# Linear attention: the output bias is added to x by GpSimd after queries and keys have unit length, and three dummy products stand in front of the first transposes

## The reference, cut to what matters

```python
x = x + _L0_attn_a_ref(_layernorm(x, axis=-1), Wq, bq, Wk, bk, Wv, bv, Wo, bo, projection)

def _spherical_features(x, projection):
    x_norm = x / (jnp.linalg.norm(x, axis=-1, keepdims=True) + 1e-08)
    return jax.nn.relu(jnp.einsum('bhsd,hfd->bhsf', x_norm, projection)) + YAT_EPS
...
Q, K, V = heads(x @ Wq + bq), heads(x @ Wk + bk), heads(x @ Wv + bv)   # 16 heads of 8
Qp, Kp = _spherical_features(Q, projection), _spherical_features(K, projection)
QKV = jnp.einsum('bhsf,bhfd->bhsd', Qp, jnp.einsum('bhsf,bhsd->bhfd', Kp, V))
normalizer = jnp.einsum('bhsf,bhf->bhs', Qp, jnp.sum(Kp, axis=2))[..., None]
out = QKV / jnp.maximum(normalizer, 1e-06)
return out.reshape(b, s, EMBED_DIM) @ Wo + bo
```

## Time and profile before

| | us |
|---|---|
| median of 3 runs | 953.96 |
| the profiled execution | 953.76 |
| its span, first to last instruction | 951.9 |
| PE busy in the span | 828.7 |
| DVE busy | 664.3 |
| ACT busy | 555.1 |
| POOL busy | 198.3 |

### The profile page before, as it was taken

One profiled execution on the slowest core, in us unless ns is written; L12 is line 12 of the kernel. 1 busy time (PEld: TensorE's weight loads), 2 busy tenths in 40 slices (PEclk: granted clock), 3 DMA queues, 4 the chain that ended last, 5 costly groups with the idle time before them and its releaser, 6 DMA issues.

```text
span 951.9 us, 17381 instructions
## 1 busy us (share of the span) xinstructions
PE 828.7 (87%) x6615; PEld 530.3 (56%) x6615; DVE 664.3 (70%) x1288; ACT 555.1 (58%) x1205; POOL 198.3 (21%) x177
## 2 busy tenths in 40 slices
PE   4889937799999889999999999999995899895894
PEld 2579735599956543333333333333575598594694
DVE  5855884266567999999999999992427364566362
ACT  2451542155525856999999888899644254423252
POOL 2000037455500050000000000000112454205385
PEclk9999957999999999999999999999996799995897
DMA  4750001321130000000000000000230212000444
GB/s 122 200 142 1 1 14 48 106 67 35 38 91 1 1 1 1 2 1 2 1 2 2 1 2 1 2 2 1 89 91 15 90 39 75 2 1 31 125 36 71
DMA packets 54643, 36.86 MB, mean 39 GB/s; under 512 B 9138, under 2 KB 50162, under 8 KB 54546
## 3 DMA queue, kind: packets, MB, share of 16 engines
q1 hardware_dynamic: 47218, 25.98, 9.8%
q0 software_dynamic: 7344, 9.77, 4.4%
HBM read 22.31 MB, written 14.48 MB: 39 GB/s over the span
## 4 chain that ended last, share of the span: by engine, by line
DVE 33%; PE 32%; POOL 14%; issue 11%; DMA 4%; ACT 4%; SPq 1%; POOLq 0%; DVEq 0%; ACTq 0%
DVE arena L1634 22%; POOL slots L1147 7%; POOL results L1158 5%; PE psum L1718 4%; PE psum L1687 2%; POOL results L1169 2%; PE psum L1251 2%; ACT arena L1898 2%; PE psum L280 2%; PE psum L402 2%; PE psum L380 2%; PE psum L1781 2%; PE psum L1769 1%; PE psum L1616 1%; PE psum L440 1%
## 5 line engine op out<-in xcount | busy, mean ns | idle before, releaser
L1634 DVE TENSOR_REDUCE arena<-psum 128x2 f32<-128x1024 f32 x256 | 294.1, 1220 | 8.6 <-PE psum L1616 8.6
L1898 ACT ACTIVATE arena<-psum 128x512 f32<-128x512 f32 x512 | 266.7, 606 | 18.9 <-PE psum L1687 16.7
L1294 ACT ACTIVATE arena<-psum,arena 128x128 f32<-128x128 f32 x340 | 97.2, 369 | 122.2 <-PE psum L1261 65.7
L1718 PE MATMUL psum<-arena 128*32 128x256 f32 (+1 forms) x1920 | 159.6, 405 | 0.2 <-ACT expert_w L1879 0.2
L1687 PE MATMUL psum<-arena 32*128 32x512 f16 x512 | 127.3, 384 | 1.8 <-ACT arena L1898 0.4
L287 PE MATMUL psum<-la_wqkv,ident 128*128 128x384 f32 x336 | 123.5, 518 | 2.4 <-ACT arena L1998 2.0
L1616 PE MATMUL psum<-arena 32*128 32x512 f16 x512 | 100.6, 384 | 17.1 <-DVE arena L1634 15.1
L1147 POOL DMA_INDIRECT slots<-xn,arena x64 | 66.4, 1038 | 196.0 <-DVE arena L1371 177.4
L1251 PE MATMUL psum<-arena 128*128 128x128 f32 x680 | 97.0, 288 | 0.7 <-DVE arena L1452 0.6
L287 PEld LDWEIGHTS psum<-la_wqkv,ident 128*128 128x128 f32 x336 | 65.1, 202 | 52.2 <-issue 15.4
L1261 PE MATMUL psum<-arena 128*128 128x128 f32 x680 | 89.9, 275 | 1.0 <-ACT arena L1294 1.0
(11 more groups left out here) (279 smaller groups left out, 1074.7 us busy)
## 6 DMA issues: line engine op xcount, KB each, us to landing
arena<-slots SPq DMA_DIRECT2D x19, 256.0 KB, 3.0
arena<-results SPq DMA_DIRECT2D x12, 256.0 KB, 4.0
slots<-blank SPq DMA_DIRECT2D x1, 2560.0 KB, 11.8
expert_w<-in_L_attn_b_w_dram SPq DMA_DIRECT2D x1, 2048.0 KB, 8.4
expert_w<-in_L_attn_b_w_dram SPq DMA_DIRECT2D x8, 256.0 KB, 4.9
expert_w<-in_L_ffn_W_dram SPq DMA_DIRECT2D x1, 2048.0 KB, 8.6
expert_w<-in_L_ffn_W_dram SPq DMA_DIRECT2D x8, 256.0 KB, 5.0
results<-arena POOLq DMA_INDIRECT x85, 2.3
```

What stands on the lines that cost most here:

```text
L1294: last = nc.scalar.activation(self.hT[:, p, c, :], ps[:, 2 + p, c * P:(c + 1) * P], self.func, bias=own[:, FF + c:FF + c + 1])
L1634: v.tensor_reduce(self.mx[:, h % 2, keys, qt, 2 * pair:2 * pair + 2], core.psum[:, 2 * slot:2 * slot + 2, :], AX.X, ALU.max).then_inc(self ...
L1718: last = nc.tensor.matmul(core.psum[32 * j:32 * j + 32, 7, cols], self.vs[:, b * TB + kt, HG * g + j, :], self.prob[:, k % self.PROBS, j, ...
L1898: nc.scalar.activation(self.prob[:, k % self.PROBS, j, :], core.psum[:, 4 + tile % self.SCORE_BANKS, :], ACT.Exp).then_inc(self.prob_in, 1)
```

## The change

Two edits, both in the linear attention.

```diff
@@ LinearAttention.tensor
         for b in range(B):
             if b == 0:
                 pe.wait_ge(w.first_in, w.first_all)
+                keep_busy(core, w, pe, self.t[0]["qkv"][0].bank, 3)
             for g, turn in enumerate(self.t[b]["xT"]):
@@ LinearAttention.gpsimd
         nc.gpsimd.memset(self.qkv[:, :, 384:400], 1.0).then_inc(self.ones, 1)
         pool.wait_ge(w.first_in, w.first_all)
+        pool.wait_ge(self.unit, B)
         for b in range(B):
             pool.wait_ge(self.normed, b + 1)
             pool.wait_ge(core.late_in, self.late + b + 1)
```

## The result

In 20 runs of each kernel on one chip, the changed kernel took 950.32 us (median; 948.08 to 954.45) and the kernel before 952.84 (950.71 to 955.81). The ratio is 0.9969, 95% interval 0.9959 to 0.9979: 0.3% faster, 2 to 4 us. The forecast was 950.9, a gain of 3.07 on 953.96; the measured gain, 2.5 between the medians and 3.0 by the ratio, lies at its size. The profiled execution's span went from 951.9 to 948.9.

The account below looks back on a forecast made before the run. The prediction took the chain of waits in the first 50 us as the bound, with DVE's stall and TensorE's slow clock. Terms -2.17, +1.29, -2.19 made -3.07: 953.96 to 950.9, range 949.5 to 954.6.

Parts of the forecast that it names:

- The stall at line 174: DVE's small operation for b = 1 is held 2.17 us by GpSimd's addition; moving the additions removes that.
- GpSimd's new place at no cost: The moved additions run beside DVE's feature evictions (line 574); price bounded at 0 to 4.7 us, taken as 0.
- Rival 4: GpSimd's additions do hold the feature evictions: +4.7 us in place of 0, so 955.6; chance 0.04.
- The dummies' start: Dummies start on PE at about 10.46, after the last first load lands, and end at 14.0.
- The clock's rise: TensorE goes to its upper level at about 13.7, between 13.3 and 14.9, during the dummies.
- the first product at 14.0 + 1.37: After the dummies end at 14.0, fast transposes take 1.37 to the first product: 15.37, rounded down to 15.3.
- The products' own term: The first sequence's 16 product records run at the fast pace and take 5.23 us.
- the third term: Clock earlier: first product to PE free for b = 1 shrinks from 7.42 to 5.23 us, -2.19.
- The sum as three terms: GpSimd moved -2.17, dummies in front of the transposes +1.29, clock earlier -2.19; together -3.07 us.
- Rival 1: The clock doesn't rise before the products and rises as late as before: gain 0.1, 953.8; chance 0.22.
- Rivals 2 and 3: Later slow stretches lengthen: one place loses 1.65 us (952.5, chance 0.12), or all three lose 4.95 (955.9, chance 0.05).
- Rival 5: Moving the additions doesn't remove the stall at line 174, clock still rises early: gain 2.19, 951.8; chance 0.02.

Follow-up runs that it names:

- dummies_only: The changed kernel without the GpSimd edit, leaving only the three dummies in front of the transposes; ratio to the kernel before 0.9988 (0.9972 to 1.0005).
- pool_only: The changed kernel without the three dummies, leaving only GpSimd's additions waiting for the unit step; ratio to the kernel before 0.9965 (0.9948 to 0.9982).
- unit_one: The changed kernel, but GpSimd's additions wait for the unit step of the first sequence only; one execution, no ratio.
- pool_again: The same kernel as pool_only, run a second time beside the changed kernel; ratio to the kernel before 0.9963 (0.9946 to 0.9980).
- early_copy2: The same kernel as early_copy, run again; ratio to the kernel before 0.9942 (0.9921 to 0.9963).
- early_copy: The changed kernel with dummies waiting for the first four loads only and ACT's second root behind the first sequence's copies; ratio to before 0.9943 (0.9921 to 0.9964).

## Why the prediction was right, point by point

One reading of the old chain was loose and carries nothing: the last bias addition starts at 30.41 and ends at 30.96.

**The stall at line 174** was read rightly: 2.17 predicted, gone in every kernel with the GpSimd edit, back in dummies_only. pool_only's first product at 13.92 is 2.26 earlier.

**GpSimd's new place at no cost** was right. The feature evictions take 2.48 in both traces. Rival 4, 4.7 us, did not occur; the evictions read PSUM and no second SBUF input, which fits what unit_one shows.

**The dummies' start** was 10.24 for a predicted 10.46, and their stretch ended at 14.24, when the transposes began, for 14.0. The near hit hides an error: from the start it is 4.00 us, more than the 3.54 of the forecast and the 3.84 of six slow records. All six records were slow, as the weight loads 0.64 us apart up to the last show:

```profile
12.32 0.33 PEld L287 LDWEIGHTS psum<-la_wqkv,ident 128*128 128x128 f32 x1 [0.31 <-issue]
12.96 0.33 PEld L287 LDWEIGHTS psum<-la_wqkv,ident 128*128 128x128 f32 x1 [0.31 <-issue]
13.60 0.23 PEld L280 LDWEIGHTS psum<-ident,xn 128*128 128x128 f32 x1 [0.31 <-issue]
```

**The clock's rise** is the step that was mis-sized. The prediction had it at about 13.7, inside the dummies, and at 14.9 at the latest, so that all transposes would be fast: 1.0 us. It came at 15.16, among the transposes, and between 14.95 and 16.14 in the five traces. They took 1.49, in other executions 1.91, 1.27, 1.83 and 1.69, between fast (1.04) and slow (1.94). The term "the first product at 14.0 + 1.37" was 15.97 instead of 15.3: 0.24 by the dummies and the rest by slow transposes. The products' own term, 5.23, came out at 15.97 to 21.24, 5.27. So the gain at that point was 2.36 for 3.07. The 24 dummy records behind begin at 27.84 for a predicted 27.1. I had drawn 13.7 from stretches of the old trace, each begun at one moment only; the same kernel's rise moves between executions, and beyond the range that I gave it. That it still came by the first product is what saved the third term.

**The sum as three terms** (-2.17, +1.29, -2.19) was right as arithmetic for both edits, but it hides what the experiments showed: the dummies' two terms together were put at -0.90, and are 0 at the first scatter (131.69 and 131.91 without them, 131.71, 131.73 and 131.57 with them). The reason lies in the old trace's slow stretch. I compared the fast products with the one execution that I had, 7.42 us, and a start 2 us earlier could have fast records too: pool_only had 6.46. At PE's release the dummies, on top of the GpSimd edit, range from a loss of 1.02 (21.24 against pool_only's 20.22) to a gain of 0.16 (against pool_again's 21.40).

**Rival 1**, no rise before the products, was nearer than its 0.22 says. Its first half came true in the changed trace: slow dummies to 14.24 (it had 14.30), the copy at 15.33 (15.45), the first product at 15.97 (16.07). Its second half, a rise as late as before, did not occur in five traces, but in dummies_only the rise stands 0.01 us behind the first product. **Rivals 2 and 3**, later slow stretches that get longer: the sign that they keep their lengths failed. The stretch that was slow from 181.00 to 184.30 before reads 0.50 from 175.70 to 182.30 in the changed trace. More than half of that lies in front of the mixture's start, where PE waits for a transfer; the start kept 2.02 of the 2.37 (181.34 to 179.32), no loss of 1.65 is seen, and the whole is not slower. **Rival 5** is excluded by line 174's 0.17.

That the measured ratio gives 3.0 where the trace holds 2.37 up to 134 us is inside its interval (2.0 to 3.9 us). Whether later stages add something is not shown, so that the time met the forecast's 3.07 so closely is in part luck.

## What to carry to other kernels

A short operation that takes ten times its usual length in one of its two places is worth a look at what the other engines run at that moment: DVE operations with two SBUF inputs and GpSimd's reads exclude each other, and an elementwise addition that nobody waits for can be put beside PSUM evictions at no cost. Dummy products warm TensorE only at a profit where PE is idle anyway: let them wait for the loads that they read themselves, and not for the last of a group, and count what they push back. Two edits that shorten the same stretch should each be measured alone: here either one had nearly the pair's gain at the first scatter, and in whole executions the GpSimd edit alone measured like the pair. And a stretch whose pace depends on the clock's rise should be traced more than once before a gain is read from it.

## What the runs showed that I had not expected

TensorE's level can fall while PE is busy. In pool_only everything was 3.38 us ahead of the kernel before until 119 us (30.20 to 26.82 for the dummies behind the second sequence), and 2.39 at the first scatter. The 1.0 us went in one line, the products of 8 columns:

```profile
116.02 4.63 PE L1200 MATMUL psum<-arena,xnT 128*128 128x8 f32 x32
```

In the kernel before and in the changed one the same 32 records take 3.64. The stretches of pool_only around it (columns as in the earlier trace rows, with all engines' busy time):

```profile
114.00:118.40 4.40, 4.40 (x39) 4.18 (x39) 4.21 (x24) 3.34 (x5) 0.00 (x0) 1.00 0.02 4
118.50:121.00 2.50, 2.15 (x11) 2.05 (x10) 0.72 (x3) 1.97 (x6) 0.00 (x0) 0.50 0.00 0
```

PE had been busy without a gap, with transposes and these narrow products, when the granted clock went to 0.50. The fall itself is no peculiarity of pool_only. The kernel before reads 1.00 up to 122.90 and 0.50 from 123.00, just as its 32 records end, and the changed one 0.50 from 121.00, 0.3 us behind their end; there it costs these records nothing. What differs is whether the records are still running. In early_copy2 the level reads 0.50 from 116.90 on, with PE still busy in them, and they take 4.34, and its lead over early_copy, 0.59 at PE's release, becomes a lag of 0.14 at the first scatter. So pool_only gave its microsecond back 100 us later, and it and the changed kernel met at 131.7.
